# A decoder layer on one core: polynomial on three engines, residual sums in SBUF, eight PSUM banks for all jobs, V in 128x32 blocks, new orders

## What is computed

```python
def polymax(x):                       # after the causal mask
    lin = jnp.where((x >= -100.0) & (x <= 0), -0.01 * x + 1.0, 0.0)
    poly = jnp.where(x > 0, x ** 2 + 1.0, 0.0)
    return (poly + lin) / 1000.0
...
x = layernorm(x + attn(x, W_attn, W_proj))        # 16 heads of 8, polymax in place of softmax
x = layernorm(x + xattn(x, ctx, WQ, WK, WV, WO))  # 16 heads of 64, softmax, keys and values from ctx
x = layernorm(x + ffn(x, router_w, expert_w))     # 16 experts, the best 6 weighted, no activation
```

## Time and profile before

| what | value |
|---|---|
| median of 3 runs | 1041.87 us |
| lowest, highest | 1039.82, 1042.03 us |
| span of the profiled execution | 1038.7 us |
| granted TensorE clock, mean | 0.994 |
| from one V to the next V on PE in the middle | 31.06 us |
| busy: PE, DVE, ACT, POOL | 96%, 93%, 73%, 38% |
| DMA, mean share of 16 engines | 8.4% |

### The profile page before, as it was taken

The page is one execution under the profiler, slowest core; times in us unless marked ns, Lnnn a source line. Parts: engine busy times, 40 slices in busy tenths (PEclk is TensorE's granted clock), DMA queues, the critical chain, the costliest instruction groups (busy, mean ns, idle before and its releaser), DMA issues.

```text
span 1038.7 us, 44351 instructions
## 1 busy us (share of the span) xinstructions
PE 995.9 (96%) x16344; PEld 862.0 (83%) x16344; DVE 969.5 (93%) x3176; ACT 757.5 (73%) x1606; POOL 391.8 (38%) x681
## 2 busy tenths in 40 slices
...
DMA packets 29576, 25.14 MB, mean 24 GB/s; under 512 B 2528, under 2 KB 24544, under 8 KB 29536
## 3 DMA queue, kind: packets, MB, share of 16 engines
...
...
## 4 chain that ended last, share of the span: by engine, by line
PE 80%; DVE 11%; issue 4%; ACT 2%; SPq 1%; POOL 1%; DMA 0%; DVEq 0%; ACTq 0%; POOLq 0%
PE ps_B L430 62%; PE ps_S L430 10%; PE ps_B L557 6%; DVE qm_lo L921 3%; DVE kp_lo L928 2%; DVE stats L780 1%; DVE ps_B L935 1%; PE ps_B L516 1%; PE ps_B L580 1%; SPq L396 1%; DVE sums L856 1%; DVE logit L880 0%; DVE rowmax L799 0%; DVE mv L786 0%; DMA xT<-in_x_t 0%
## 5 line engine op out<-in xcount | busy, mean ns | idle before, releaser
L856 DVE SCALAR_TENSOR_TENSOR sums<-ps_B,gate,sums 128x128 f32<-128x128 f32 x896 | 236.9, 341 | 2.2 <-PE ps_B L430 2.2
L997 POOL TENSOR_TENSOR p<-p,rowinv 128x1024 f32<-128x1024 f32 x64 | 121.9, 1905 | 193.6 <-DVE rowinv L812 193.6
L987 POOL TENSOR_TENSOR rstd<-mv,ln_eps_tile 128x2 f32<-128x2 f32 x96 | 18.7, 195 | 383.0 <-DVE mv L786 383.0
L627 ACT ACTIVATE q2T<-ps_B 128x512 f32<-128x512 f32 x128 | 76.0, 596 | 77.3 <-PE ps_B L430 74.1
L653 ACT ACTIVATE relu<-ps_B 128x512 f32<-128x512 f32 x128 | 73.1, 599 | 73.2 <-PE ps_B L430 72.8
L430 PE MATMUL ps_B<-wo_sb,oT 128*128 128x128 f32 x1024 | 122.8, 278 | 0.0
L627 ACT ACTIVATE p2T<-ps_B 128x512 f32<-128x512 f32 x128 | 76.9, 603 | 59.5 <-PE ps_B L557 58.1
L430 PEld LDWEIGHTS ps_B<-wo_sb,oT 128*128 128x128 f32 x1024 | 116.7, 192 | 2.4 <-DVE sums L856 0.3
L430 PE MATMUL ps_B<-ex_hi,x2T_hi 128*128 128x512 f32 x256 | 110.4, 431 | 1.2 <-POOL x2T_lo L971 0.8
L735 ACT ACTIVATE x<-ps_B,shift,rstd 128x128 f32<-128x128 f32 x192 | 78.4, 469 | 37.7 <-POOL shift L992 37.7
L430 PE MATMUL ps_B<-ex_hi,x2T_lo 128*128 128x512 f32 x256 | 102.0, 399 | 0.0
...
## 6 DMA issues: line engine op xcount, KB each, us to landing
xT<-in_x_t SPq DMA_DIRECT2D x32, 256.0 KB, 2.7
...
```

What stands on the lines that cost most here:

```text
L627: return nc.scalar.activation(dst, src, ACT.Copy, scale=scale)
L856: done = V.scalar_tensor_tensor(after, ps[BANK[f"FF{4 * r + q}"]][:, C * e:C * e + C], gate[:, r, 4 * q + e:4 * q + e + 1], before, ALU.mu ...
L997: G.tensor_tensor(weights, weights, rowinv[:, r].unsqueeze(2).broadcast_to([P, H, T]), ALU.mult).then_inc(p2_ready, 1)
```

## The change

**Lags.** A turn no longer has four stages. Each job and step has its own lag, the tile that it works on less the turn's number, from 0 for the experts (-1 for the third norm) to 4 for Q, K, S1 and V (5 for the load of x). Full turns are 1 to 26.

**Banks.** PSUM is four pairs of banks. A job takes one bank (B0 to B7) or a pair (P0 to P3), the same in each turn, and every job has its own `full` and `emptied`. PE waits for the bank's last occupant, found from the lists.

**Polynomial.** ACT has a third step `u` (`line_of`), 1 - 0.01 x from PSUM into the new SBUF tile `line`. `allow` now frees the bank. `pieces` is the larger of square + 1 and `line`, in SBUF. `p1_` is a plain product on POOL. It waits for `pieces`, `allow` and for the last Y.

**Residual sums.** `projected`, `attended` and the last `weigh` write the new SBUF tiles `residual1` to `residual3` and free the bank themselves. `stats` and `norm` read these tiles.

**V.** Sixteen matmuls of 128x32 tiles in place of eight of 128x64.

**Orders.** All lists are new. Only their first lines stand in this cut of the diff:

```diff
-    ("V2_0", "B2", "l2"), ("S2_0", "S", "l2"), ("Y", "B4", "l1"), ("X2T", "B3", "ff"), ("Q", "B1", "s1"),
...
+    ("PR", "B0", 2), ("X2T", "B3", 0), ("K2_1", "B2", 2), ("Q", "B5", 4), ("V2_2", "B3", 2),
+    ("LG", "B0", 0), ("PT1a", "B1", 1), ("PT1b", "B4", 1), ("K", "B2", 4), ("AC0", "P3", 1),
...
+    "DVE": """
+        projected@2 stats3@-1 stats1@2 logits@0 gate0@0 gate1@0 var1@2 queries_lo@4 var3@-1 pieces2@3 gate2@0 gate3@0 keys_lo0@4
...
-            ps[b] = ctx.enter_context(nc.psum_tensor("ps_" + b, [P, 1024 if b == "S" else 512], F32))
-        full = {b: sem("full_" + b) for b in BANKS}
-        emptied = {b: sem("emptied_" + b) for b in BANKS}
...
+        pairs = [ctx.enter_context(nc.psum_tensor(f"ps_{n}", [P, 1024], F32)) for n in range(4)]
+
+        def ps(job):
+
+            banks = banks_of("WO0" if job == "WO1" else job)
+            return pairs[banks[0] // 2][:, 512 * (banks[0] % 2):512 * (banks[0] % 2) + 512 * len(banks)]
+
...
+        residual = {n: sb(f"residual{n}", [P, NR, C]) for n in (1, 2, 3)}
...
+            with eng.Fori(FIRST_TURN + 1, LAST_TURN + 1) as turn:
+                for name, lag in STEADY[engine]:
+                    IN_LOOP[:] = range(FIRST_TURN + 1 + lag, LAST_TURN + 1 + lag)
+                    do(name, turn + lag)
...
-                    for b in range(NB):
-                        for par in range(2):
-                            last = mm(ps[BANK["V"]][64 * par:64 * par + 64, T * b:T * b + T], xT[:, b, 0], w_v[:, par])
...
+                    for par in range(2):
+                        for half in range(2):
+                            rows = 64 * par + 32 * half
+                            last = mm(ps("V")[rows:rows + 32, T * b:T * b + T], xT[:, b, 0, 32 * half:32 * half + 32], w_v[:, par])
...
+            def relu_of(tile, b):
+                wait_full(act, f"S1_{b}", tile)
+                wait(act, p1_ready, NB * tile + b - 1)
+                nc.scalar.activation(relu[:, b % 2], ps(f"S1_{b}"), ACT.Relu).then_inc(relu_ready, 1)
+
+            def line_of(tile, b):
+
+                wait_full(act, f"S1_{b}", tile)
+                wait(act, poly_ready, NB * tile + b - 1)
+                copy(line[:, b % 2], ps(f"S1_{b}"), -0.01, 1.0).then_inc(line_ready, 1)
...
-                def allow(b):
-
-                    if b >= 2:
-                        wait_emptied(dve, i, f"S1_{b - 2}")
-                    elif not (isinstance(i, int) and u == 0):
-                        wait_emptied(dve, i - 1, f"S1_{b + 2}")
-                    dve.wait_ge(relu_ready, NB * u + b + 1)
-                    V.scalar_tensor_tensor(allowed[:, b % 2].rearrange("p (j n) -> p j n", j=J), ps[BANK[f"S1_{b}"]][:].rearrange("p (j n) -> p j n", j=J), -100.0,
-                                           causal.unsqueeze(1).broadcast_to([P, J, T]), ALU.is_ge, ALU.mult).then_inc(allowed_ready, 1)
-
-                def pieces(b):
-
-                    dve.wait_ge(square_ready, NB * u + b + 1)
-                    dve.wait_ge(allowed_ready, NB * u + b + 1)
-                    V.scalar_tensor_tensor(ps[BANK[f"S1_{b}"]][:], ps[BANK[f"S1_{b}"]][:], -0.01, relu[:, b % 2], ALU.mult, ALU.max).then_inc(poly_ready, 1)
-
-                def p1_of(b):
-                    dve.wait_ge(poly_ready, NB * u + b + 1)
-                    seqs, heads = slice(b // 2 * 2, b // 2 * 2 + 2), slice(b % 2 * NV * T, b % 2 * NV * T + NV * T)
-                    V.scalar_tensor_tensor(p1[:, seqs, heads], ps[BANK[f"S1_{b}"]][:].rearrange("p (s n) -> p s n", s=2), 1.0,
-                                           allowed[:, b % 2].rearrange("p (s n) -> p s n", s=2), ALU.add, ALU.mult).then_inc(emptied[BANK[f"S1_{b}"]], 1)
-
...
+            def allow(tile, b):
+
+                dve.wait_ge(line_ready, NB * tile + b + 1)
+                wait(dve, p1_ready, NB * tile + b - 1)
+                V.scalar_tensor_tensor(allowed[:, b % 2].rearrange("p (j n) -> p j n", j=J), ps(f"S1_{b}").rearrange("p (j n) -> p j n", j=J), -100.0,
+                                       causal.unsqueeze(1).broadcast_to([P, J, T]), ALU.is_ge, ALU.mult).then_inc(emptied[f"S1_{b}"], 1)
+
+            def pieces(tile, b):
+
+                dve.wait_ge(square_ready, NB * tile + b + 1)
+                dve.wait_ge(line_ready, NB * tile + b + 1)
+                V.scalar_tensor_tensor(relu[:, b % 2], relu[:, b % 2], 1.0, line[:, b % 2], ALU.add, ALU.max).then_inc(poly_ready, 1)
...
+            def p1_of(tile, b):
+
+                pool.wait_ge(poly_ready, NB * tile + b + 1)
+                wait_emptied(pool, f"S1_{b}", tile)
+                wait_full(pool, "Y", tile - 1)
+                seqs, heads = slice(b // 2 * 2, b // 2 * 2 + 2), slice(b % 2 * NV * T, b % 2 * NV * T + NV * T)
+                G.tensor_tensor(p1[:, seqs, heads], relu[:, b % 2].rearrange("p (s n) -> p s n", s=2),
+                                allowed[:, b % 2].rearrange("p (s n) -> p s n", s=2), ALU.mult).then_inc(p1_ready, 1)
...
+            def projected(tile):
+
+                wait_full(dve, "PR", tile)
+                dve.wait_ge(x_in, 16 * (tile + 1))
+                wait(dve, normed[1], tile)
+                V.tensor_tensor(residual[1][:].rearrange("p r c -> p (r c)"), ps("PR")[:, 0:NR * C], x_sb[:].rearrange("p r c -> p (r c)"), ALU.add).then_inc(emptied["PR"], 1)
...
+            def attended(tile):
+
+                wait_full(dve, "WO1", tile)
+                dve.wait_ge(x1b_ready, tile + 1)
+                wait(dve, normed[2], tile)
+                V.tensor_tensor(residual[2][:].rearrange("p r c -> p (r c)"), ps("WO1")[:, 0:NR * C], x1b[:].rearrange("p r c -> p (r c)"), ALU.add).then_inc(emptied["WO0"], 1)
...
+                        if q == 3 and e == 3:
+                            after = residual[3][:, r]
...
+            def norm(tile, n):
+                dst = {1: x1, 2: x2, 3: x3}[n]
+                if n == 1:
+                    wait(act, x1b_ready, tile)
+                    wait_full(act, "X1T", tile - 1)
+                elif n == 2:
+                    wait(act, base3_ready, NR * tile)
+                    wait_full(act, "X2T", tile - 1)
+                else:
+                    wait(act, out_done, 16 * tile)
+                act.wait_ge(ln_shift[n - 1], tile + 1)
+                for r in range(NR):
+                    last = nc.scalar.activation(dst[:, r], residual[n][:, r], ACT.Identity, bias=shift[:, n - 1, r:r + 1], scale=rstd[:, n - 1, r:r + 1])
```

More of the change, by code:

```diff
@@ L63 @@
 JOBS = [
[10 rows of a table removed]
[9 rows of a table added]
 ]
 BANK = {job: bank for job, bank, _ in JOBS}
-BANKS = ["B0", "B1", "B2", "B3", "B4", "B5", "S"]
-SP_ORDER = """
-    x_columns x_rows store context
-""".split()
-ACT_ORDER = """
-    V2_0 Y X2T queries_hi exp0 logit_exp K V2_2 norm1 V2_1 V2_3 V relu0 x1_hi relu1 K2_0 K2_3 square0 Q2_3 K2_1 exp1
-    PT0b square1 K2_2 PT0a base3 Q2_2 PT1a PT1b AC0 relu2 relu3 AC1 square2 square3 Q2_1 Q2_0 norm3 norm2
-""".split()
-DVE_ORDER = """
-    row_max0 less_max0 projected logits stats1 gate0 var1 gate1 queries_lo gate2 keys_lo0 gate3 keys_lo1 gate4
-    row_sum0 gate5 row_max1 gate6 row_inv0 x1_lo gate7 allow0 gate8 less_max1 gate9 pieces0 gate10 p1_0 gate11
-    allow1 gate12 gate13 row_sum1 gate14 row_inv1 gate15 pieces1 weigh0 p1_1 weigh1 weigh2 weigh3 stats3 allow2 var3
-    allow3 pieces2 pieces3 attended stats2 var2 p1_2 p1_3
@@ L130 @@
     "SP": """
-        store@NT-2 store@NT-1 x_rows@NT-2 context@NT-2 store@NT
+        x_rows@-2 context@-1 x_rows@-1 store@-6 store@-5 store@-4 store@-3 store@-2 store@-1
     """,
     "PE": """
-        V2_0@NT-2 S2_0@NT-2 Y@NT-2 X2T@NT-2 V2_1@NT-2 PR@NT-2 V2_2@NT-2 V2_3@NT-2 LG@NT-2 S2_1@NT-2 K2_0@NT-2 FF0@NT-2
-        K2_3@NT-2 X1T@NT-2 K2_1@NT-2 PT0b@NT-2 K2_2@NT-2 Q2_3@NT-2 PT0a@NT-2 FF4@NT-2 FF1@NT-2 Q2_2@NT-2 AC0@NT-2 PT1a@NT-2
-        Q2_1@NT-2 FF5@NT-2 PT1b@NT-2 FF2@NT-2 FF6@NT-2 FF3@NT-2 AC1@NT-2 FF7@NT-2 WO0@NT-2 WO1@NT-2 Q2_0@NT-2 S2_0@NT-1
@@ L750, in _, with do @@
+            def do(name, tile):
+                if name[:3] == "mPT":
+                    move_p2T(tile, name[3:])
+                else:
+                    step, args = chosen(steps, name)
+                    step(tile, *args)
+            turns(act, do, "ACT")
         @block.vector
```

1081 lines of the change are left out of this document (538 added, 543 removed), and 16 rows, old and new, of the table JOBS.

## The result

| what | before | after |
|---|---|---|
| median | 1041.7 us | 1057.84 us |
| lowest, highest | 1039.82, 1042.03 us | 1056.58, 1058.92 us |
| span of the profiled execution | 1038.7 us | 1056.9 us |
| granted TensorE clock, mean | 0.994 | 0.983 |
| V to V on PE in the middle, mean | 31.05 us | about 30.75 us |

The account below looks back on a forecast made before the run. PE was taken as the bound: 31.06 - 0.68 - 0.45 - 0.03 + 0.40 = 30.3 us a turn; 32 turns plus 44.8 and 2 us of ends gave 1016.4 span, 1019.5 us time, range 1003 to 1038.

Parts of the forecast that it names:

- The bound of the kernel before: PE bounds the turn of 31.06 us, of which 0.68 us are waits, read from start times on PE.
- Boundaries and V: On PE, 12 tile-shape boundaries become 8, 0.45 us a turn less; V in 128x32 blocks saves 0.03.
- New waits: PE waits newly before X1T (about 0.2 us) and Q2_0 (0 to 0.2): 0.4 us a turn, bounds 0 and 1.1.
- POOL and DVE in each other's way: Rival, chance 0.03: each `pieces` on DVE waits for a POOL product; DVE needs 33.1 us, time about 1109.
- POOL's product: Each 128x512 product for `p1` on POOL takes 1.13 us, four a turn, costing nothing under PE's cover.
- The loop over the last norm: Slower rival, chance 0.06: `attended` late on DVE delays the next turn's Q; at 2.3 us late, 1064 us.
- SP's queue: `x_columns`, behind `context`, lands 30.2 us into the turn, just in time for `next_x_hi`, and costs nothing.
- Lags and ends: Fill of five tiles, ACT leading with 92 us, PE 86, and drain: 2 us added, bounds -6 and +15.
- rival of a longer fill: ACT's 92 us don't overlap with the start and its in-order waits add up: +13 us, 1032.5, chance 0.06.
- signs of being wrong that I had named: PE wait over 0.5 us before X1T, Q2_0 or Q; `pieces` over 1 us; DVE never idle; first full turn after 115.

Follow-up runs that it names:

- kernel with three edits: Changed kernel with V of tile 1 later in the fill, SP loading x columns before context, POOL's unit-2 product waiting for `x1_lo`: 1033.1 us, ratio 0.9916.
- experiment 5: Changed kernel, but in the loop of full turns POOL's `p1` product for unit 2 waits until `x1_lo` is done: 1039.2 us, ratio 0.9973.

## Why the prediction was wrong

**The bound of the kernel before: right.** The wait before V that was read from start times is the one that the view of waits names (0.27 of the 0.68 us a turn), and it is gone. The other 0.41 no view names. They were read from start times alone, and the turn of 29.90 below bears them out.

**Boundaries and V: right.** 31.06 - 0.68 - 0.45 - 0.03 = 29.90 was to be the turn without waits. The kernel with three edits has a turn of 29.90 with 0.02 of waits. That it agrees to a hundredth is partly luck: a boundary was known as 0.08 to 0.13, and V came at 0.56 and not 0.58. Y and V now have the same shape, and no step stands between them (64 records in 0.92 us, then V's 32 in 0.56 with the boundary behind it):

```profile
516.65 1.10 PE L432 MATMUL ps<-p,vp 128*32 128x64 f32 x64
517.57 0.63 PE L432 MATMUL ps<-w_attn_sb,xT 128*32 128x64 f32 x32
518.13 0.39 PE L432 MATMUL ps<-qm_hi,kp_hi 64*128 64x256 f32 x2
```

**New waits: the size was too small.** The term was 0.40 us a turn (bounds 0 and 1.1), "Q2_0 late by 0 to 0.2". It is 0.85 (30.75 - 29.90), with Q2_0 late by 0.65 and X1T not late. That is within the bounds I kept, and costs 26 x 0.45 = 11.7 us. With this term and the ends both at their upper bounds my sum would have given 1019.5 + 22.4 + 13 = 1054.9, yet the range stopped at 1038. I had walked ACT's queue to `x1_hi` and given DVE's `x1_lo` no queue of its own, while gates 10 to 14 stand right ahead of it.

**POOL and DVE in each other's way: the mechanism was named, its price and place were not.** The rival had 0.03, since it was costed as throughput: four `pieces`, 5.6 us a turn, DVE as the bound. One of four `pieces` collides (1.06 against 0.68 us) and DVE is not the bound. What counted is the latency of one small instruction on the way to PE: 0.97 us of `gsum`. The sentence with which I left this rival out of the sum (no row has both at once in such a size) asked about large instructions only. Moving the product out of its way gave 18.7 us, more than the whole loss in the middle against the forecast. DVE was to be busy 27.5 us a turn and was busy 29.7 (289.65 of 300 us). `gsum` and the one `pieces` explain 1.35 of the 2.2, the rest I can't place: in experiment 5, without the long `gsum`, it is still 28.9.

**POOL's product** takes 1.29 us, not the 1.13 that lay between the neighbouring shapes. On the path only as part of the 1.12 above.

**The loop over the last norm: not seen.** In none of these kernels does PE wait before Q in the middle.

**SP's queue: nearly right.** It was to be just in time. The columns came 0.5 us late for `next_x_hi`, and `shares1` behind it made PT1a wait. Removing it alone gave little, as the loop was held elsewhere.

**Lags and ends: the step that failed.** "I add 2 us, bounds -6 and +15" is the term. With turns of 30.75 it measured 1056.9 - 32 x 30.75 - 44.8 = 28.1 us, outside its own bounds. (The 28.8 above counts the same loss with six turns of the sum laid into the ends.) The first full turn began at 126.4 us, not 106, and PE's waits up to there are 17.2 us more than before. I summed the work of each engine and found ACT's 92 us the largest. To that I added some 14 us in which it is idle, about as much as in today's fill (62.5 us of which ACT is busy 46.6 and PE 48.1). The new fill:

```profile
0.00:126.40 126.40, 94.97 (x1576) 81.38 (x1577) 81.17 (x181) 93.24 (x187) 62.24 (x76) 0.93 0.17 52
```

ACT's 93.2 us are as counted, but it is idle for 33 us and not 14, and taking 12 us of work away from it changed little. So the step that failed is the assumption that a fill of five tiles leaves its fullest engine no more idle time than one of three. ACT didn't lead either: PE was busy 95.0 us where I had counted 86. Part of that is the lower clock in two stretches, of which this is the longer:

```profile
17.20:27.40 10.20, 6.16 (x63) 5.24 (x64) 2.58 (x4) 3.84 (x9) 4.46 (x6) 0.51 0.25 72
```

In this stretch and the one from 30.9 to 37.7 us PE is busy 10.25 us at half its clock. At the full one that work would take some 5 us less (an estimate from these rows), and before, the whole fill ran at 1.00. How much of the 5 is on the path was not tried. The rival of a longer fill had 0.06 and +13 us, so its chance and its size were both too small.

The drain holds the other 8.4 us. PE's waits after 900 us grew from 9.1 to 13.7 us in all, and those that hang on the weighted sums account for it, before and after:

```profile
PE ps_B L430 <- DVE sums L856: 0.4, 1, 0.4
```

```profile
PE ps L432 <- DVE sums L867: 4.9, 5, 2.3
```

The longest, at 1047.23 us, stands among the experts of the last tile, which follow each other with nothing between them. The other four are matmuls of the tiles before it that wait for a bank. No experiment changed the drain.

Of the signs of being wrong that I had named, three came: a wait over 0.5 us before Q2_0, a `pieces` longer than 1 us (one in four), and a first full turn after 115 us.

**What stays open.** Of the 20 us of fill over the forecast, the polynomial's instructions carry 3.8 to 5.6 by experiment and the late V of tile 1 some 1.8 to 3.6. These may overlap. The rest is only read from the waits: a few tiles in flight, each step waiting for the one before, and no expert jobs to put between. None of that was tried, nor were the lower clock and the drain. So for most of the 28 us the cause is argued and not shown. In the kernel with all three edits too, the ends take 1033.6 - 26 x 29.90 = 256.2 us, as long as in the changed one.
